# A closing product by parts, a last group in halves, a dummy gate and a reordered beginning

## The reference

```python
x = x + layernorm(first(layernorm(x)))        # a linear layer trained token by token (a scan over 2048 steps)
x = x + layernorm(second(layernorm(x)))
# second: six times
x = attention(shift(x), Wqkv, q_scale, k_scale, Wo) + x   # 16 heads of 64, windows of 32 keys, rotary tables
x = ffn(shift(x), ln_g, ln_b, W1, b1, W2, b2) + x         # layer norm, a * gelu(gate), 341 hidden features
# ffn
a, gate = split(layernorm(x) * g + bln) @ W1 + b1)
return a * gelu(gate) @ W2 + b2
```

## Time and profile before

| | |
|---|---|
| Median of three runs | 1494.74 us (1492.25 to 1496.88) |
| The profiled execution's own time | 1491.09 us |
| Its span | 1489.3 us |
| PE, DVE, POOL, ACT busy | 96%, 89%, 81%, 78% |
| Loop with all stages (172 to 1426 us), PE busy | 1246.96 of 1254 us |
| Beginning, 72 to 140 us | PE waits often, and its clock is at times half of full |
| End, from 1458 us | DVE, POOL and ACT take turns with PE |

### The profile page before, as it was taken

How to read it: one execution, slowest core, us unless ns; L and a number is a source line. 1 busy time by engine, 2 the same in 40 slices (tenths; PEclk the granted TensorE clock), 3 DMA queues, 4 the chain that set the end, 5 groups by cost and what they waited for, 6 DMA issues and landing times.

```text
span 1489.3 us, 74807 instructions
## 1 busy us (share of the span) xinstructions
PE 1436.4 (96%) x32908; PEld 784.4 (53%) x32908; DVE 1328.3 (89%) x1795; ACT 1161.7 (78%) x2288; POOL 1208.7 (81%) x1047
## 2 busy tenths in 40 slices
PE   7978999999999999999999999999999999999996
PEld 6823544555545545555555545545555555555553
DVE  5578999989999989999999999989999999999975
ACT  4337888878888888888888888888888888888882
POOL 6158999888888888888888888888888888888951
PEclk9979999999999999999999999999999999999999
DMA  6000000010000020000020000020000000000000
GB/s 209 18 14 31 3 10 11 8 62 10 3 20 15 4 66 11 3 20 16 3 67 11 4 19 16 3 66 11 3 11 24 4 10 11 3 10 25 3 11 30
DMA packets 24260, 32.67 MB, mean 22 GB/s; under 512 B 2323, under 2 KB 21120, under 8 KB 23040
## 3 DMA queue, kind: packets, MB, share of 16 engines
q1 hardware_dynamic: 23936, 27.88, 5.8%
HBM read 20.80 MB, written 1.05 MB: 15 GB/s over the span
## 4 chain that ended last, share of the span: by engine, by line
PE 90%; DVE 5%; issue 2%; POOL 1%; ACT 1%; DMA 0%; POOLq 0%; DVEq 0%; ACTq 0%
PE psq L271 23%; PE ring L293 21%; PE ring L323 11%; PE pss L312 10%; PE ring L281 9%; PE ring L337 8%; PE ring L347 4%; PE ring L370 1%; DVE qa L889 1%; PE ring L406 1%; DVE qb L905 1%; DVE qb L1024 1%; DVE mx L1046 0%; ACT sq L1277 0%; PE ring L468 0%
## 5 line engine op out<-in xcount | busy, mean ns | idle before, releaser
L293 PE MATMUL ring<-mh,x0S 128*32 128x512 f32 x3072 | 408.3, 595 | 0.0
L271 PE MATMUL psq<-wqk,x0S 128*32 128x512 f32 x3072 | 393.1, 608 | 6.8 <-ACT sq L1277 4.7
L1423 POOL TENSOR_TENSOR qa<-qa,qb 128x1024 f32<-128x1024 f32 x96 | 229.5, 2390 | 6.7 <-DVE qb L1024 6.7
L1482 POOL TENSOR_TENSOR qa<-qa,qb 128x1024 f32<-128x1024 f32 x96 | 228.4, 2379 | 0.0
L323 PEld LDWEIGHTS ring<-u,pT 128*32 128x32 f32 x6144 | 170.6, 110 | 62.3 <-issue 57.8
L1464 POOL TENSOR_TENSOR pr<-pr,rden 128x1024 f32<-128x1024 f32 x96 | 183.8, 1915 | 13.8 <-DVE rden L924 13.8
L323 PE MATMUL ring<-u,pT 128*32 128x128 f32 x6144 | 191.0, 273 | 3.6 <-ACT uT L1262 1.8
L271 PEld LDWEIGHTS psq<-wqk,x0S 128*32 128x32 f32 x3072 | 94.2, 111 | 182.8 <-issue 164.6
L1443 POOL TENSOR_TENSOR qa<-qa,rn 128x1024 f32<-128x1024 f32 x96 | 182.7, 1903 | 0.2
L1459 POOL TENSOR_TENSOR qa<-qa,rn 128x1024 f32<-128x1024 f32 x96 | 182.7, 1903 | 0.0
L312 PEld LDWEIGHTS pss<-kT,qT 64*32 64x32 f32 x12288 | 134.4, 105 | 89.7 <-issue 82.3
(11 more groups left out here) (186 smaller groups left out, 2721.2 us busy)
## 6 DMA issues: line engine op xcount, KB each, us to landing
wqk<-in_wqk SPq DMA_DIRECT2D x6, 1024.0 KB, 8.5
mvT<-in_mvT SPq DMA_DIRECT2D x6, 512.0 KB, 3.8
wo<-in_wo SPq DMA_DIRECT2D x6, 512.0 KB, 5.4
xf<-x SPq DMA_DIRECT2D x23, 128.0 KB
xf<-x SPq DMA_DIRECT2D x23, 127.0 KB
rope<-in_rope SPq DMA_DIRECT2D x1, 2048.0 KB, 10.2
w<-in_w SPq DMA_DIRECT2D x6, 341.0 KB, 2.9
xmid<-in_x SPq DMA_DIRECT2D x4, 256.0 KB, 3.8
```

Of the source, the lines that this page charges most:

```text
L271: last = mm(psq[WIN * w:WIN * w + WIN, 512 * (n % 2):512 * (n % 2) + 512], x0S[:, tile * P + WIN * w:tile * P + WIN * w + WIN], wqk[:, l % ...
L293: last = mm(bank[WIN * g:WIN * g + WIN, :], x0S[:, tile * P + WIN * w:tile * P + WIN * w + WIN], mh[:, l % 2, g, :, :].rearrange("p j n -> ...
L1423: g_.tensor_tensor(qa[:, t % 2, 1024:2048], qa[:, t % 2, 1024:2048], qb[:, 1024:2048], ALU.add).then_inc(sum_k, 1)
L1482: g_.tensor_tensor(qa[:, t % 2, 0:1024], qa[:, t % 2, 0:1024], qb[:, 0:1024], ALU.add).then_inc(sum_q, 1)
```

## The change

It has five parts.

1. Beginning, PE and ACT: `features(0)` goes ahead of `apply_v(3)`; `merge((2, 3), 0)` moves into step 0, behind `chain_d(4)`. ACT's copies follow: `applied` is parted in two, `featured(0)` comes between `applied_x(3)` and `applied_v(3)`.
2. Beginning, POOL: the tables of tiles 0 and 1 come ahead of the roots of `layer_norm(0, 0)`.
3. End, ACT: in body 2, behind the last Exp and ahead of the copy of the last values (L1253), a gelu of one column into a new tile `warm`.
4. End, PE: `contract(22)` is parted. Blocks 0 and 1 (32 products) run in body 6 as soon as the product of block 1 (`A1`) is there, block 2 (16 products) behind the transposes of group 23. `contract(23)` is parted too, in two halves of two tiles with a bank each: blocks 0 and 1 of half a, of half b, block 2 of half a, of half b.
5. End, the others: DVE, POOL and SP do the last group in halves of two tiles: both sums and statistics, both roots, both norms, two stores. The norm of group 22 keeps its place ahead of them.

```diff
+def narrow(bank, tiles=(0, 1, 2, 3), parts=(0, 1, 2)):
+    for k in tiles:
+        for j in parts:
...
+def contract_begin(i, half):
+    bank, n = take("Z" + half, i)
+    abank, m = place["A1", i]
+    pe.wait_ge(freed[abank], m + 1)
+    wait(pe, freed[bank], n)
+    narrow(ring[bank], HALF[half], (0, 1))
+def contract_end(i, half):
+    bank, n = place["Z" + half, i]
+    abank, m = place["A2", i]
+    pe.wait_ge(freed[abank], m + 1)
+    narrow(ring[bank], HALF[half], (2,)).then_inc(filled[bank], 1)
...
             apply_x(3)
+            features(0)
             apply_v(3)
-            merge((2, 3), 0)
             wait(pe, s_lmask, 1)
             wait(pe, s_uz, 1)
-            features(0)
...
                     halves_turned([ring[bank] for bank, n in banks], lambda blk: xh[:, blk * P:blk * P + P], QUAD)
+                    if i == ALLG - 1:
+                        contract_end(i - 1, "")
...
+                if i == ALLG - 2:
+                    contract_begin(i, "")
+                if i == ALLG - 1:
+                    contract_begin(i, "a")
+                    contract_begin(i, "b")
+                    contract_end(i, "a")
+                    contract_end(i, "b")
...
+                if s == 0:
+                    merge((2, 3), 0)
...
+                if s == STEPS + 10:
+                    for half in range(2):
+                        last_sum(half)
+                    for half in range(2):
+                        last_norm(half)
...
             merged(1)
-            applied(3)
+            applied_x(GROUPS - 1)
+            featured(0)
+            applied_v(GROUPS - 1)
             merged(2)
             merged(3)
-            featured(0)
...
                 if s == STEPS + 2:
+                    nc.scalar.activation(warm[:, :], eps[:, 0:1], ACT.Gelu)
...
+            wait(pool, s_tables, 16 * NTABLES)
+            for t in range(2):
+                table(t)
             layer_norm(0, 0)
             layer_norm(0, 1)
-            wait(pool, s_tables, 16 * NTABLES)
```

More of the change, by code:

```diff
@@ L62, in norm_at @@
 def norm_at(s):
-    bodies = [STEPS + n for n in (6, 7, 10, 14)]
+    bodies = [STEPS + n for n in (6, 7, 10)]
     return LASTG + bodies.index(s) if s in bodies else -1
+HALF = {"": (0, 1, 2, 3), "a": (0, 1), "b": (2, 3)}
 def chunk_at(s, j):
@@ L89, in build @@
         ident_pad = sb("ident_pad", [P, 2 * P])
+        warm = sb("warm", [P, 1])
         ident = ident_pad[:, 1:1 + P]
@@ L338, in hidden @@
                 return last
[L340 to L344, removed]
+            def narrow(bank, tiles=(0, 1, 2, 3), parts=(0, 1, 2)):
+                for k in tiles:
+                    for j in parts:
+                        n = HBLK[j][1] + (j == 2)
                         for w in range(NWIN):
@@ L347, in narrow @@
                             last = mm(bank[rows, k * P:k * P + P], uT[0:n, j, k * P + WIN * w:k * P + WIN * w + WIN],
-                                      w2[0:n, j, :], start=(j == 0), stop=(j == 2))
+                                      w2[0:n, j, :], start=(j == 0 and (k == tiles[0] or len(parts) == 3)),
+                                      stop=(j == 2 and (k == tiles[-1] or len(parts) == 3)))
                 return last
@@ L641, in _ @@
                 i = feed_at(s, 15, (6, 10))
-                if i >= 0 and i != ALLG - 3:
+                if 0 <= i < ALLG - 3:
                     contract(i)
+                if i == ALLG - 2:
[5 more added lines that the diff above has]
+                    contract_end(i, "b")
                 i = feed_at(s, 14, (5, 9))
@@ L799, in gate_first, with last_sum, last_norm @@
                                        uT[0:rows, 0, :], ALU.add, ALU.mult).then_inc(freed[bank], 1)
+            def last_sum(half):
+                bank, n = place["Z" + "ab"[half], ALLG - 1]
+                dve.wait_ge(filled[bank], n + 1)
+                tiles = slice(TILES - QUAD + 2 * half, TILES - QUAD + 2 * half + 2)
+                v.tensor_tensor(x0T[:, tiles, :].rearrange("p k (a n) -> p k a n", a=2),
+                                ring[bank][:, 2 * half * P:2 * half * P + 2 * P].rearrange("p (k a n) -> p k a n", k=2, a=2),
+                                x1[:, :, 1 + tiles.start:1 + tiles.stop, :].rearrange("p a k n -> p k a n"), ALU.add).then_inc(freed[bank], 1)
+                dve.wait_ge(freed[bank], n + 1)
+                for k in (2 * half, 2 * half + 1):
+                    last = v.bn_stats(fbst[:, k, :], x0T[:, TILES - QUAD + k, :])
+                last.then_inc(f_stats, 1)
+                dve.wait_ge(f_stats, 2 * GROUPS - 1 + 2 * half)
+                for k in (2 * half, 2 * half + 1):
+                    last = v.bn_aggr(fmv[:, GROUPS - 1, k, :], fbst[:, k, :])
+                last.then_inc(f_stats, 1)
+            def last_norm(half):
+                dve.wait_ge(f_rstd, GROUPS + half)
+                for k in (2 * half, 2 * half + 1):
+                    tile = x0T[:, TILES - QUAD + k, :]
+                    last = v.tensor_scalar(tile, tile, fmv[:, GROUPS - 1, k, 0:1], frstd[:, GROUPS - 1, k:k + 1], ALU.subtract, ALU.mult)
+                last.then_inc(f_norm, 1)
+                dve.wait_ge(f_norm, GROUPS + half)
+                tiles = slice(TILES - QUAD + 2 * half, TILES - QUAD + 2 * half + 2)
+                v.tensor_tensor(xmid[:, tiles, :], x0T[:, tiles, :], xmid[:, tiles, :], ALU.add).then_inc(f_out, 1)
             def result(u):
@@ L936, in _ @@
                 i = group_at(s, 16)
-                if i >= LASTG:
+                if LASTG <= i < ALLG - 1:
                     g = i - LASTG
@@ L1129, in applied @@
                 cp(x0S[:, 512 * g + 1:512 * g + 513], ring[bank][:, :]).then_inc(freed[bank], 1)
-            applied(0)
-            applied(1)
-            applied(2)
+            for g in range(GROUPS - 1):
+                applied_x(g)
+                applied_v(g)
             merged(0)
             merged(1)
-            applied(3)
+            applied_x(GROUPS - 1)
+            featured(0)
+            applied_v(GROUPS - 1)
             merged(2)
             merged(3)
-            featured(0)
             wait(act, s_lmask, 1)
@@ L1388, in layer_norm, with table @@
                       lnmr[:, j, 0:size], l_rs[j], 3 * u - 2).then_inc(l_nmr[j], 1)
+            def table(t):
+                wait(pool, rope_k, t - 1)
+                wait(pool, rope_q, t - 1)
+                g_.tensor_tensor(tab[:, t % 2, :, :].rearrange("p a d -> p (a d)"), rope[:, t % TILES, :],
+                                 qk_scales[:, t // TILES, :], ALU.mult).then_inc(tab_ready, 1)
             for g in range(GROUPS):
@@ L1433, in _ @@
                 t = s - 0
[L1434 to L1438, removed]
+                if 2 <= t < STEPS:
+                    table(t)
                 t = s - 3
@@ L1445, in _ @@
                 i = group_at(s, 20)
-                if i >= LASTG:
+                if i == ALLG - 1:
+                    g = GROUPS - 1
+                    for half in range(2):
+                        part = slice(2 * half, 2 * half + 2)
+                        pool.wait_ge(f_stats, 2 * GROUPS + 2 * half)
+                        g_.tensor_tensor(fvare[:, g, part], fmv[:, g, part, 1:2].rearrange("p k o -> p (k o)"), eps[:, part],
+                                         ALU.add).then_inc(f_var, 1)
+                        pool.wait_ge(f_var, GROUPS + half)
+                        g_.tensor_tensor(frstd[:, g, part], fvare[:, g, part], neg_half[:, part], ALU.pow).then_inc(f_rstd, 1)
+                if LASTG <= i < ALLG - 1:
                     g = i - LASTG
@@ L1555, in _ @@
                 i = group_at(s, 18)
-                if i >= LASTG:
+                if i == ALLG - 1:
+                    for half in range(2):
+                        tiles = slice(TILES - QUAD + 2 * half, TILES - QUAD + 2 * half + 2)
+                        sp.wait_ge(f_out, GROUPS + half)
+                        sp.dma_start(out_v[:, tiles, :], xmid[:, tiles, :]).then_inc(s_out, 16)
+                if LASTG <= i < ALLG - 1:
                     g = i - LASTG
```

7 lines of the change are left out of this document (4 added, 3 removed).

## The result

| | before | after |
|---|---|---|
| Median | 1493.49 us (4 runs, 1491.12 to 1496.88) | 1482.93 us (4 runs, 1479.99 to 1484.29) |
| Profiled execution, its span | 1491.09, 1489.3 | 1479.99, 1477.9 |

The ratio is 0.9939, 95% interval 0.9926 to 0.9952, so -9.1 us (-11.0 to -7.2); the two medians themselves lie 10.6 us apart.

The account below looks back on a forecast made before the run. PE was taken to bound the loop, busy 193.90 of 194 us, so only the two ends could gain: -2.1 + 0 - 1.1 - 1.7 - 1.9 = -6.8 us, from a median of 1494.74 to 1487.9 us; range 1484.5 to 1492.0.

Parts of the forecast that it names:

- Features first: Beginning: features ahead of the second application start the first projections 2.3 us and the second 2.05 earlier; -2.1 us, bounds -0.9 and -2.3.
- Dummy gate: End, ACT: the gelu's table loads in idle time, so the last mixing comes earlier; -1.1 us, bounds 0 and -1.28.
- Split product: End, PE: with group 22's closing product parted, group 23's transposes start 1.7 us earlier; -1.7 us, bounds 0 and -2.1.
- Last group: End: closing products start earlier, DVE and POOL overlap in halves; -1.9 us, bounds -0.9 and -2.4.
- The store: Span's end: the last store, with half the bytes, left at the 2.73 us of before.
- The rule of the Trainium skill: End: DVE and GpSimd share ports, so half a's residual sum would wait for the second power; 0.4 us later, sum -6.4.
- (a): Beginning gives nothing, as the late merge or its copies hold the square of the keys; -4.7, 1490.0 us; chance 0.13.
- (b): End gives half: the gate doesn't inherit the load, or the split product only moves the wait; 1490.7 us; chance 0.07.
- (e): Both ends come out as they were, gains run over by unseen waits; 1494.7 us; chance 0.04.
- (d): Slower: the moved beginning brings the stretch from 117 to 133 us to the lower clock; +7, 1502 us; chance 0.04.
- (c): Beginning: the denser stretch until 74.6 us saves one run of projections from the lower clock (1.7); 1486.2 us; chance 0.08.
- How the numbers follow: Closing step: chances (faster 0.79, same 0.17, slower 0.04) and range, from the terms' bounds and 2 us between single runs.

Follow-up runs that it names:

- e11: The changed kernel with the rotary tables made behind the roots as before; one execution, 1481.12 us.
- e12: The changed kernel without the dummy gate; one execution, 1485.93 us.
- e8: The changed kernel with the closing product of group 22 in one piece, ahead of the transposes of group 23; one execution, 1483.15 us.
- e6: The changed kernel with the mixing weights' load moved, without a wait, so that it went out directly behind the projection weights; median 1493.63 us of 12, ratio 1.0008.

## Why the prediction was right in its steps and wrong in its time

- **Features first, -2.1:** measured -2.34, just past the bound of -2.3. The order came as worked out. The first projections came 2.46 us earlier (2.3 forecast). The merged copies cost the square nothing (0.2 forecast); the merge cost DVE 0.11, where the prediction had it hidden with 0.05 to spare.
- **Tables first, 0:** 0 (e11).
- **Dummy gate, -1.1:** -1.05 (e12). DVE's transpose is late next, as forecast.
- **Split product, -1.7:** -1.73, half by starting at the earlier gate, half by the order (e8). The prediction's sign of it, hidden products "2.8 nearer to the last mixing", had added the dummy gate's 1.1, which moves the mixing as well; they came 1.73 nearer.
- **Last group, -1.9:** -1.97. Halves of 1.14 and 1.07 us on DVE (1.23 and 1.03 forecast).
- **The store, left at 2.73:** 2.24 or 2.25 in eleven profiles of kernels with halves. This is the term of the sum that was most mis-sized: put at nothing, it was 0.49 us for half of the bytes.
- **The rule of the Trainium skill** (SBUF — State Buffer, the shared port pair), by which the sum would have been -6.4, does not hold here for a small power beside a sum: 0.43 against 0.42 us. It does for the wide table products, 1.43 against 0.60 (e11).

The sum of the steps was -6.8; they measured -7.6, and the pooled runs say -7.8. Rivals (a), (b) and (e) are out by the stretches, (d) did not come. Rival (c), a kinder clock, gave nothing that belongs to the change: from the second projections to the first row maximum the kernels with the old beginning took 47.75, 46.53 and 46.45 us, those with the new one 46.40 to 47.81.

**The step that failed** is the one in "How the numbers follow" that gave single runs "the 2 us by which [they] differ". They differ by 11 us (1486.56 to 1497.70 in 61 runs of the kernel before); the three shown had lain within 4.6. The changed kernel's median of four (1482.93) was 1.0 us below its own mean of 16. The median of three from which the forecast started (1494.74) was 3.0 us above the mean of 61. These 4 us of chance, and the 1.0 us by which the pooled -7.8 exceeds the -6.8 of the sum, are the 5.0 us between the time and the forecast of 1487.9. The lower bounds of the terms add up to -8.3; with 4 us for chance in place of 2, the range would have begun at about 1482.4 and held the time. That the prediction tied the median to one profiled execution by its distance of 3.65 us was the same fault: that distance is scatter.

## What to carry to other kernels

Cut two traces at the same instructions and compare stretch by stretch: a stretch that a change touches repeats to 0.05 us, while whole times differ by 10, so one trace prices an edit that a dozen timed executions barely show. In an engine's end-game look for the wait that is named last at each hand-over, and fill it with a piece of the work that stands behind it: of the four pieces that gained, three came within 0.1 us of a hand calculation and the fourth within 0.25. A queue that only issues transfers has no sense of steps; moving a load in its list moves it in time only where something makes it wait.

## What was not expected of the hardware

- Waits of TensorE with no releaser in the profile, 0.2 to 2.2 us, most of them behind the layers' weight loads, and 3.8 us when two megabytes went out together (314 GB/s in 4 us). The 33 longest end 2.3 to 2.65 us after a packet on the queue of TensorE's instructions starts, as they would if it had run out of them.
- TensorE's clock in the beginning: trios of 128x512 bfloat16 products in its waits kept the granted clock at 1.00 from 76 to 108 us and saved 3.3 us net in that stretch, pairs did not keep it throughout (0.89). A fall can also come behind a dense stretch: in e8 the first two applications took 1.99 and 1.90 us and in e6 1.93 and 1.91, instead of 1.16 and 1.05, at a granted clock of 0.50 and 0.61 from 57 to 60 us, though PE had been busy 3.85 and 3.62 of the 4 us from 50 to 54; all behind was 1.6 us later.
- Storing the last 128 KB instead of 256 KB brought the end 0.49 us closer.
